# Cross-attention scores from stacked high and low halves of Q, and Q projected a whole group at a time

## What is computed

```python
qh = _split_heads(q @ wq.T + bq, h)
kh = _split_heads(k @ wk.T + bk, h)
vh = _split_heads(v @ wv.T + bv, h)
scores = jnp.einsum('ntd,nsd->nts', qh, kh) / jnp.sqrt(jnp.asarray(depth, qh.dtype))
scores = scores + km * PAD
attn = jax.nn.softmax(scores, axis=-1)
ctx = jnp.einsum('nts,nsd->ntd', attn, vh)
out = _merge_heads(ctx, h) + q
out = (out - mu) / jnp.sqrt(var + LN_EPS) * gamma + beta
```

## Time and profile before

| | |
|---|---|
| median of 3 runs | 1153.81 us (1152.42 to 1155.73) |
| the profiled execution | 1157.28 us, of which the span is 1155.5 us |
| PE busy | 1123.1 us (97%), 7541 matmuls |
| weight loads (PEld) busy | 1037.8 us (90%), 7541 loads |
| DVE busy | 822.1 us (71%) |
| ACT busy | 612.5 us (53%) |
| POOL busy | 771.8 us (67%) |
| 16 DMA engines | 40% |

### The profile page before, as it was taken

The page is one execution under the profiler, slowest core; times in us unless marked ns, Lnnn a source line. Parts: engine busy times, 40 slices in busy tenths (PEclk is TensorE's granted clock), DMA queues, the critical chain, the costliest instruction groups (busy, mean ns, idle before and its releaser), DMA issues.

```text
span 1155.5 us, 25702 instructions
## 1 busy us (share of the span) xinstructions
PE 1123.1 (97%) x7541; PEld 1037.8 (90%) x7541; DVE 822.1 (71%) x1622; ACT 612.5 (53%) x1008; POOL 771.8 (67%) x667
## 2 busy tenths in 40 slices
PE   7899999999999999999999999999999999999994
PEld 7788789999999999999999999999999999999983
DVE  5776467777777777777777777777777777777786
ACT  3321254556566555555555656655555555565551
POOL 4999523677766676766667776667676666777465
PEclk9999999999999999999999999999999999999996
DMA  7745433233343444343344333344443334333223
GB/s 228 261 147 188 150 104 90 74 122 95 116 119 117 126 126 126 116 120 99 102 123 122 106 105 119 117 126 126 126 116 122 98 102 123 123 101 110 85 82 128
DMA packets 147207, 141.07 MB, mean 122 GB/s; under 512 B 86452, under 2 KB 88004, under 8 KB 147172
## 3 DMA queue, kind: packets, MB, share of 16 engines
q1 hardware_dynamic: 146564, 140.29, 40.1%
q10 hardware_dynamic: 608, 0.33, 0.1%
HBM read 91.71 MB, written 48.85 MB: 122 GB/s over the span
## 4 chain that ended last, share of the span: by engine, by line
PE 84%; DVE 2%; POOL 1%; issue 0%; ACT 0%; DMA 0%; DVEq 0%; SPq 0%; POOLq 0%
PE q_ps L724 31%; PE o_ps L765 23%; PE s_ps L740 18%; PE t_ps L751 12%; POOL x_lo L991 0%; DVE stats L822 0%; DVE attn L853 0%; PE q_ps L765 0%; DVE y L862 0%; DMA xT_raw<-in_xT 0%; DVE attn L814 0%; DVE row_max L885 0%; DVE y L868 0%; ACT q_hi L1030 0%; DVE y L843 0%
## 5 line engine op out<-in xcount | busy, mean ns | idle before, releaser
L765 PE MATMUL o_ps<-v_tiles,pt 128*128 128x66 f32 x2520 | 310.7, 270 | 1.5 <-DVE attn L814 1.5
L765 PEld LDWEIGHTS o_ps<-v_tiles,pt 128*128 128x128 f32 x2520 | 304.0, 192 | 1.9 <-issue 1.9
L885 DVE TENSOR_REDUCE row_max<-s_ps 128x8 f32<-128x616 f32 x256 | 203.2, 794 | 118.2 <-PE s_ps L740 118.1
L740 PE MATMUL s_ps<-bd,q_hi 128*128 128x308 f32 x1024 | 260.5, 305 | 1.1 <-ACT q_hi L1030 1.1
L991 POOL TENSOR_TENSOR x_lo<-xT_raw,x_hi 128x512 fp32r<-128x512 f32 x124 | 159.3, 1286 | 117.8 <-ACT x_hi L1026 117.7
L961 POOL TENSOR_TENSOR attn<-attn,x_rows 128x512 f32<-128x512 f32 x124 | 160.2, 1292 | 115.8 <-DVE attn L814 115.8
L1036 ACT COPY pt<-t_ps 128x512 f32<-128x512 f32 (+1 forms) x320 | 175.0, 588 | 107.1 <-PE t_ps L751 107.0
L1030 ACT ACTIVATE q_hi<-q_ps,bq_col 128x512 fp32r<-128x512 f32 x125 | 86.1, 689 | 254.9 <-PE q_ps L724 254.9
L724 PE MATMUL q_ps<-x_lo,wq_hi 128*128 128x512 f32 x500 | 218.7, 437 | 2.5 <-PEq L142 2.1
L1016 ACT ACTIVATE probs<-probs 128x616 f32<-128x616 f32 x256 | 183.3, 716 | 64.3 <-DVE probs L894 64.3
L894 DVE TENSOR_TENSOR probs<-s_ps,row_max 128x616 f32<-128x616 f32 x256 | 204.6, 799 | 5.7
(11 more groups left out here) (96 smaller groups left out, 1292.9 us busy)
## 6 DMA issues: line engine op xcount, KB each, us to landing
xT_raw<-in_xT SPq DMA_DIRECT2D x128, 256.0 KB, 3.5
x_rows<-in_x SPq DMA_DIRECT2D x32, 1024.0 KB, 5.6
out<-y SPq DMA_DIRECT2D x128, 256.0 KB, 2.1
k_scratch<-k_out SPq DMA_DIRECT2D x8, 1232.0 KB, 5.4
bd<-k_scratch SPq DMA_DIRECT2D x128, 77.0 KB, 2.4
v_scratch<-v_out SPq DMA_DIRECT2D x16, 264.0 KB
v_tiles<-v_scratch SPq DMA_DIRECT2D x256, 9.9 KB
ctx_raw<-in_ctxT SPq DMA_DIRECT2D x3, 1232.0 KB, 6.2
```

The source lines that it names most:

```text
L740: mm = pe.matmul(s_ps[t % 2][:, j, 0:GS], (q_hi, q_lo)[u][:, g, P * t:P * t + P], bd[par][:, v, g, :, :].rearrange("p h s -> p (h s)"), st ...
L765: mm = pe.matmul(bank_of(b, t)[:, col:col + tile_cols[i]], pt[h][0:w, i, P * t:P * t + P], v_tiles[v_buffer(b, h)][0:w, i, 0:tile_cols[i]] ...
L885: dve.tensor_reduce(row_max[:, u, :].rearrange("p (j h) -> p j h", j=2), score_heads(t), AX.X, ALU.max).then_inc(max_ready, 1)
```

## The change

Each group of Q (four heads, 32 rows each) is now kept as two tensors, `q_pair[0]` and `q_pair[1]`. `q_pair[0]` has the high parts of heads 0 and 1 in rows 0 to 63 and their low parts in rows 64 to 127; `q_pair[1]` has the high parts of heads 2 and 3 in rows 64 to 127 and their low parts in rows 0 to 63. The high parts of K stand in `bd` a second time, 64 rows further (`twin`), so that a matmul of one `q_pair` by the high K gives hi by hi and lo by hi together, and a second one, by the low K, gives hi by lo. Each takes the two heads' 154 columns. Per group there are four matmuls of 154 columns in place of three of 308.

ACT's `high_q` and DVE's `q_low` become two instructions of 64 rows each. PE projects a whole group at every even sub-step (`q_half` twice) and nothing at odd ones. ACT's `high_q` moves to the even sub-step behind `exponent`; DVE's `q_low` of the first half stands behind `subtract_max` of the even sub-step, and that of the second half stays in the odd one. ACT's `high_x` and `norm` are spread differently over sub-steps 3 to 7. SP issues eight DMAs for `bd` in place of four.

```diff
-    KDMA = HG * DMA
+    KDMA = 2 * HG * DMA
+    HP = P // 2
...
-        q_hi = sb(whole, "q_hi", [P, NG, T], F32R)
-        q_lo = sb(whole, "q_lo", [P, NG, T], F32R)
+        q_pair = [sb(whole, f"q_pair{d}", [P, NG, T], F32R) for d in range(2)]
...
                         sp.dma_start(bd[par][rows, :, :, q, :].bitcast(F32), k_dram[b, rows, :, :, :]
                                      ).then_inc(k_loaded[par], DMA)
+                        twin = slice((DH * q + HP) % P, (DH * q + HP) % P + DH)
+                        sp.dma_start(bd[par][twin, 0, :, q, :].bitcast(F32), k_dram[b, rows, 0, :, :]
+                                     ).then_inc(k_loaded[par], DMA)
...
-                        for n, (u, v) in enumerate(terms):
-                            mm = pe.matmul(s_ps[t % 2][:, j, 0:GS], (q_hi, q_lo)[u][:, g, P * t:P * t + P],
-                                           bd[par][:, v, g, :, :].rearrange("p h s -> p (h s)"),
-                                           start=(n == 0), stop=(n == 2))
+                        for d in range(2):
+                            for v in range(2):
+                                mm = pe.matmul(s_ps[t % 2][:, j, 2 * S * d:2 * S * d + 2 * S],
+                                               q_pair[d][:, g, P * t:P * t + P],
+                                               bd[par][:, v, g, 2 * d:2 * d + 2, :].rearrange("p h s -> p (h s)"),
+                                               start=(v == 0), stop=(v == 1))
...
-                        if real(qb) and not in_phase_one(qb, g):
-                            q_half(qb, g, t % 2, (par + h) % 2)
+                        if t % 2 == 0 and real(qb) and not in_phase_one(qb, g):
+                            q_half(qb, g, 0, (par + h) % 2)
+                            q_half(qb, g, 1, (par + h) % 2)
...
+                    rows, twin = slice(HP * d, HP * d + HP), slice(HP - HP * d, P - HP * d)
+                    dve.wait_ge(q_hi_ready, b * 8 + (2 * g + d + 1))
+                    dve.scalar_tensor_tensor(out=q_pair[d][twin, g, :], in0=q_bank(b, g)[rows, :],
+                                             scalar=bq_col[rows, g:g + 1], in1=q_pair[d][rows, g, :],
+                                             op0=ALU.add, op1=ALU.subtract).then_inc(q_lo_ready, 1)
...
                         if real(a + h) and t % 2 == 1 and not in_phase_one(a + h, g):
-                            q_low(a + h, g)
+                            q_low(a + h, g, 1)
...
                             subtract_max(a, h, t)
+                        if real(a + h) and t % 2 == 0 and not in_phase_one(a + h, g):
+                            q_low(a + h, g, 0)
...
-                    act.activation(q_hi[:, g, :], q_bank(b, g)[:, :], ACT.Identity, bias=bq_col[:, g:g + 1]
-                                   ).then_inc(q_hi_ready, 1)
+                    for d in range(2):
+                        rows = slice(HP * d, HP * d + HP)
+                        act.activation(q_pair[d][rows, g, :], q_bank(b, g)[rows, :], ACT.Identity,
+                                       bias=bq_col[rows, g:g + 1]).then_inc(q_hi_ready, 1)
```

More of the change, by code:

```diff
@@ L211, in load_keys @@
                         sp.dma_start(bd0[rows, :, :, q, :].bitcast(F32), k_dram[b, rows, :, :, :]).then_inc(k_loaded[0], DMA)
+                        twin = slice((DH * q + HP) % P, (DH * q + HP) % P + DH)
+                        sp.dma_start(bd0[twin, 0, :, q, :].bitcast(F32), k_dram[b, rows, 0, :, :]).then_inc(k_loaded[0], DMA)
                 def store_values(c, first, end):
@@ L370, in _ @@
                     act.wait_ge(q_done, g + 1)
-                    act.activation(q_hi[:, g, :], k_ps[g][:, :], ACT.Identity, bias=bq_col[:, g:g + 1]
-                                   ).then_inc(q_hi_ready, 1)
+                    for d in range(2):
+                        rows = slice(HP * d, HP * d + HP)
+                        act.activation(q_pair[d][rows, g, :], k_ps[g][rows, :], ACT.Identity, bias=bq_col[rows, g:g + 1]
+                                       ).then_inc(q_hi_ready, 1)
             @block.vector
@@ L718, in q_half @@
                             used -= 1
-                        at_least(pe, q_hi_ready, used)
-                        at_least(pe, q_lo_ready, used)
+                        at_least(pe, q_hi_ready, used * 2)
+                        at_least(pe, q_lo_ready, used * 2)
                     x_part = (x_hi[par], x_lo[par])
@@ L1045, in step @@
                         h, t = s // 4, s % 4
-                        if 3 <= s <= 6 and real(a + 2):
+                        if s in (4, 6) and real(a + 2):
                             high_x(a + 2, s - 3, par)
-                        g = (2 if h == 0 else 0) + t // 2
-                        if t % 2 == 1 and real(a + h) and not in_phase_one(a + h, g):
-                            high_q(a + h, g)
                         if s == 0:
@@ L1056, in step @@
                             exponent(a, (s - 1) // 4, (s - 1) % 4)
+                        g = (2 if h == 0 else 0) + t // 2
+                        if t % 2 == 0 and real(a + h) and not in_phase_one(a + h, g):
+                            high_q(a + h, g)
                         if real(a - 1 + h):
@@ L1059, in step @@
                                 copy_pt(a - 1 + h, 1 - h, i)
-                        if 3 <= s <= 6 and real(a - 2) and not is_last(a - 2):
-                            norm(a - 2, s - 3, par)
+                        if s in (3, 5) and real(a + 2):
+                            high_x(a + 2, s - 3, par)
+                        if real(a - 2) and not is_last(a - 2):
+                            if s in (3, 5, 7):
+                                norm(a - 2, (s - 3) // 2, par)
+                            if s == 7:
+                                norm(a - 2, 3, par)
                 steps(act, step)
```

20 lines of the change are left out of this document (9 added, 11 removed).

## The result

| | before | after |
|---|---|---|
| median | 1154.05 us (1152.42 to 1155.73, 4 runs) | 1241.71 us (1240.55 to 1244.70, 4 runs) |
| PE busy | 1123.1 us (97%) | 1167.4 us (94%) |
| DVE busy | 822.1 us (71%) | 938.1 us (76%) |
| ACT busy | 612.5 us (53%) | 720.9 us (58%) |

The changed kernel takes 1.076 times as long (95% interval 1.074 to 1.079), 87.7 us more. The prediction was +45 us and at most 1214: the direction is right, the forecast size is half of what came, and the time lies outside the range.

What follows compares the result with a forecast made beforehand. PE was taken as the bound, its matmuls paced by weight loads. Scores 10.6 us, waits 33.5 and the first part's end 0.6 gave +45 us, from 1153.8 to 1199 us; forecast 1190 to 1212 (chance 0.60), range 1160 to 1214.

Steps and rivals of the forecast that it cites:

- The bound and its rule: PE alone sets the steady pace; each matmul costs the larger of its columns and the next weights' load, 0.112 us.
- +0.33: Scores on PE: eight load-bound matmuls of 0.112 us a sub-step in place of six wide ones, +0.33 us a batch.
- B: Rival for PE's scores: loads keep the columns' pace, but DVE's chain stays; +0.18 us a batch, 1160 us; chance 0.08.
- C: Rival: scores keep the columns' pace and DVE's halves cost half, so the kernel gets faster, 1112 us; chance 0.04.
- D: Rival for PE's scores: narrow float32r matmuls cost more a column, 1227 us (chance 0.04), or 1472 with two passes (0.08).
- The place of the cost: PE waits for DVE's scale at sub-steps 1 and 5, and for q_ps at 2 and 0: +1.08 us a batch.
- Rival A: Load-bound scores but little waiting, as DVE's halves cost half or its chain is shorter: 1169 us, up to 1185; chance 0.13.
- the chain's size: DVE's chain from PE's finished scores to the next product: 3.29 us against 2.89 of PE work, so 0.40 waiting.
- 0.66 for the added half q_low: DVE's chain, from the added half's start to the next instruction: 0.66 us, as long as a whole q_low.
- the 0.72 ahead of it: DVE's chain, from the subtraction's start to the next instruction's start: 0.72 us.
- "Does not wait" at 3 and 7: Products of sub-steps 3 and 7: PE has 3.33 us of work against DVE's 3.29 us chain, so no wait.
- Other engines: ACT, DVE's total load, POOL and SP's extra DMAs do not become the bound: nothing taken, at most 1 us in all.

Runs made afterwards that it cites:

- e8: Changed kernel with the score matmuls by the low K streaming 76 columns in place of 154: 1239.08 us, ratio 1.073.
- e2: Kernel before, with only PE's whole-group projection and ACT's changed order; single 128-row q_low stays in the odd sub-step: 1157.98 us, ratio 1.002.
- e11: Same as e1, but both q_low on rows 0 to 63, each waiting only for its own ACT half: 1173.92 us, ratio 1.017.
- e1: Changed kernel's pairs and halves, but half a group projected every sub-step, ACT's old order, both q_low in the odd sub-step: 1180.53 us, ratio 1.023.
- e3: Same as e2, but the single 128-row q_low stands in the even sub-step behind subtract_max: 1189.51 us, ratio 1.030.
- e4: Changed kernel with both halves of q_low in the odd sub-step: 1230.74 us, ratio 1.066.
- e5: Changed kernel with both q_low on all 128 rows, into tiles of their own: 1200.36 us, ratio 1.038.
- e6: Changed kernel with both q_low on 64 rows, always from row 0, into tiles of their own: 1199.83 us, ratio 1.038.
- e7: Same as e6, but both q_low on 64 rows, always from row 64: 1241.51 us, ratio 1.075.
- e10: Kernel before with four more DMAs a batch of the size of bd's, into a spare tile: 1154.19 us, ratio 0.998.

## Why the prediction was right and wrong

**The bound and its rule held; that the part came out at +0.35 against +0.33 is luck.** PE sets the pace, and a matmul costs the larger of its columns and the next load: there is a load to each matmul (8053 of each), and e8 shows that columns below the load's time are worth next to nothing. But eight narrow scores were to take 0.896 everywhere, 0.112 each. They take 0.85 behind a projection, no more than the six wide ones, and the 0.94 behind a product is there with wide ones too (e2), paid for by the projections. With what they slow behind them they cost 0.13 a batch in the change (0.35 - 0.33 + 0.11) and 0.13 to 0.15 in e11 and e1, near the +0.14 that the prediction had for 0.109 a load. So this term was some 0.2 us a batch, 6 us, too high. Rivals B, C and D fall all the same: B and C need eight scores in 0.59 us, D in 1.05 or more. By the 81 ns of the Trainium skill's page "TensorE: Matmul & The Clock Gate", section "Back-to-back issue gap", the eight would take 0.65, an estimate; the trace does not agree, with 0.85.

**The place of the cost held.** The waits are where the prediction had them, 64 for the product's bank behind DVE's scale and those for `q_ps` behind the second half. e2, e3 and e4 show it from three sides: whole groups alone cost 2 us, `q_low` ahead of the scale some 34, and both halves in the odd sub-step only move the waits. Rival A falls: the halves are 685 and 749 ns long, as the wholes.

**The step that failed is the chain's size: "0.66 for the added half q_low", with the 0.72 ahead of it.** Those distances were taken from the earlier trace rows, from a 128-row `q_low` between instructions of the same start row. The half has them as 0.83 and 0.78. It is one term mis-sized by 0.11 and 0.12, in a chain that has no slack, and the same holds for the half in front of `q_ps`. e5 and e6, without it, are at 1200.36 and 1199.83: the prediction's 1199 was the time of a kernel whose halves start at row 0. Start rows are 41 to 44 us, and 43 were missed; e6 against e7 shows it. That e6 meets the 1199 to a microsecond is in part luck: in its trace the waits are 1.25 us a batch where 1.08 was predicted, and the rest 0.13 where it was 0.33. The prediction had asked of the halves only how long they are, not where they start.

**Two smaller terms were low, and one was high.** From maximum to subtraction it took 0.83, while the range in its own text went to 0.93; with the BN_AGGR of sub-step 1 it is 0.93 (604.29 to 605.22). From reciprocal to scale it took 0.23, from the kernel's end; at this place it is 0.33 (606.83 to 607.16), and was so before the change too (629.75 to 630.08 in the same trace as the earlier trace rows). Against these 0.20 us stand 0.17 at the end: from the scale's end to the load it took 0.06 (607.58 to 607.64) in place of 0.12, and the matmul's record starts with the load's, not 0.11 later. So the wait at sub-step 1 is 0.40 + 0.23 (start rows) + 0.20 - 0.17 = 0.66, as measured in this batch.

**"Does not wait" at 3 and 7 failed by the same term.** 3.29 against 3.33 left 0.04 us of room, and the start rows take 0.23. In the change these products wait 0.15 and 0.14 in the batch shown; in e6, with the halves from row 0, they wait 0.00 on average over the loop. And a product that begins behind a wait takes longer itself: 1.13 and 1.14 to the next start in the table's sub-steps 3 and 5, in place of 1.04. Its first load then has no matmul to hide behind, as I read it. These 0.1 us a wait were in no term.

**The parts do not add.** The pairs alone are 26 us (e1) and `q_low` ahead of the scale is 34 (e3), 60 together against 88. In the change one half is in the chain to the product and the other in that to `q_ps`, each with the two sides of its start row. I did not split these 28 us further.

**Other engines**: nothing, as predicted, for the DMAs (e10) and for ACT's order (e2). POOL has a new place in the list of waits (DVE's `attn` for `y`, 35.2 us), harmless: e2 has more of it, 55.2, and costs 2 us. The profile also books 24.8 us of waits of the product's loads to ACT's copies (`pt`). But the product of an odd sub-step needs no copy that the one before it did not need too, and at such a wait (the load at 641.75 us) DVE's scale had ended 0.12 us before, as in the waits that are booked to DVE.

## What to carry to other kernels

Splitting a 128-row instruction in two halves of 64 doubles its time on VectorE and ScalarE, and on VectorE a half that starts at another row than its neighbours costs about 0.115 us more on each side; put such steps where the chain to the bounding engine has room, or let all start at the same row. When a measured part equals the forecast, look at its neighbours too: 0.33 us had only changed its owner here. Before columns of a matmul are saved, look at the distance of its loads: below some 250 columns here, an estimate from 0.112 us a load and 0.44 ns a column, there should be nothing left to save; measured is that 76 columns in place of 154 in half of the score matmuls saved 2.6 of 1242 us (e8). Where a forecast says that a chain of eight distances just fits (3.29 in 3.33), the range has to hold the case in which it doesn't.

## What was not expected of the hardware

- The overlap of 83 ns between neighbours on VectorE turns into a gap of 31 to 33 ns when the start row changes, and again when it changes back (e6 against e7). Without the change of start row, 64 rows and 128 rows behave alike.
- After PE has waited, its next group of ten matmuls takes 0.09 us more (mean 1.12 in place of 1.04; 1.13 and 1.14 in the batch shown). Whatever comes behind a product on PE, wide scores, narrow ones or a projection, takes 0.08 us more than elsewhere.
- Four float32r matmuls of 76 columns and four of 154 take 0.81 to 0.89 us, 0.10 to 0.11 each, about the distance of the loads alone; what follows them takes back the 0.04 us that they save.
